# A gated graph layer on one core: the edges' scan cut into sixteen parts and placed in other units, the edge table's later steps moved

## What is computed

```python
h = relu(layernorm(x))
u = h @ root + bias
for r in range(8):
    mask = (edge_type == r)
    sums = segment_sum(h[src] * mask, dst)      # one row per node
    cnt  = segment_sum(mask, dst)
    u = u + (sums / max(cnt, 1)) @ weight[r]
z = concat([u, h]) @ w_gate + b_gate
out = x + tanh(u) * z + h * (1 - z)
```

## Time and profile before

| | |
|---|---|
| time, three runs | 1409.28, 1410.62, 1416.18 us; median 1410.62 |
| the profiled execution: span from the first to the last instruction | 1407.7 us |
| busy: TensorE matmuls | 1291.5 us, 92% of the span |
| busy: VectorE | 952.5 us, 68% |
| busy: GpSimd | 754.8 us, 54% |
| busy: ScalarE | 409.0 us, 29% |
| the chain that ended last, by engine | PE 61%, DVE 13%, DMA 10%, issue 7%, POOL 4%, ACT 2% |

### The profile page before, as it was taken

One profiled execution on the slowest core, in us unless ns is written; L12 is line 12 of the kernel. 1 busy time (PEld: TensorE's weight loads), 2 busy tenths in 40 slices (PEclk: granted clock), 3 DMA queues, 4 the chain that ended last, 5 costly groups with the idle time before them and its releaser, 6 DMA issues.

```text
span 1407.7 us, 20144 instructions
## 1 busy us (share of the span) xinstructions
PE 1291.5 (92%) x6205; PEld 651.6 (46%) x6205; DVE 952.5 (68%) x1260; ACT 409.0 (29%) x501; POOL 754.8 (54%) x837
## 2 busy tenths in 40 slices
PE   2978899999999999999998999998999989786898
PEld 1434344444444445555554445454445445343565
DVE  6889678366565667775675577646666778765777
ACT  5344123214132422321332043223222323432000
POOL 2423088786878426686687558664756464320000
PEclk9998899999999999999999999999999999998999
DMA  6442125215224348777875887769889977648872
GB/s 220 154 173 101 44 52 156 69 45 171 54 59 122 114 158 277 238 237 247 277 209 161 292 267 246 238 210 305 279 254 303 312 230 240 204 138 248 239 226 90
DMA packets 112355, 269.44 MB, mean 191 GB/s; under 512 B 22558, under 2 KB 23061, under 8 KB 112268
## 3 DMA queue, kind: packets, MB, share of 16 engines
q1 hardware_dynamic: 78284, 185.88, 40.2%
q0 software_dynamic: 33984, 82.40, 20.4%
HBM read 203.66 MB, written 87.30 MB: 207 GB/s over the span
## 4 chain that ended last, share of the span: by engine, by line
PE 61%; DVE 13%; DMA 10%; issue 7%; POOL 4%; ACT 2%; DVEq 1%; SPq 1%; POOLq 1%; ACTq 0%
PE ps L1320 52%; PE ps L1278 8%; DMA early<-y_rows,pair 7%; DVE W L937 2%; DMA early<-u_rows 1%; POOL onehot L641 1%; DVE hT L990 1%; DMA W<-in_L_gnn_weight_dram 1%; POOL early L633 1%; DVE hT L985 1%; PE ps L1313 1%; POOL pair L623 1%; DVE early L1147 1%; DVE early L1069 1%; DVE early L1163 1%
## 5 line engine op out<-in xcount | busy, mean ns | idle before, releaser
L1320 PE MATMUL ps<-W,hT 128*128 128x512 f16 (+2 forms) x4740 | 1076.0, 385 | 13.0 <-DVE W L937 13.0
L1320 PEld LDWEIGHTS ps<-W,hT 128*128 128x128 f16 (+2 forms) x4740 | 479.9, 104 | 537.8 <-issue 43.4
L633 POOL DMA_INDIRECT early<-y_rows,pair x200 | 242.1, 1211 | 194.5 <-PE ps L1281 152.4
L606 POOL DMA_INDIRECT table_rows<-edges,table_i x160 | 240.5, 1503 | 100.6 <-issue 100.6
L1278 PE MATMUL ps<-early,onehot 128*125 x800 | 205.9, 385 | 26.6 <-POOL onehot L641 13.1
L641 POOL TENSOR_SCALAR onehot<-iota_d,pair 128x125 f16<-128x125 f16 x185 | 159.9, 864 | 64.2 <-DMA early<-y_rows,pair 58.2
L766 ACT ACTIVATE yhl<-early 128x512 f16<-128x512 f32 x120 | 75.3, 628 | 355.3 <-DVE early L1069 194.2
L937 DVE SCALAR_TENSOR_TENSOR W<-W,wsc 128x2048 f16<-128x2048 f32 x62 | 146.5, 2364 | 13.8 <-ACT W L716 13.7
L1278 PEld LDWEIGHTS ps<-early,onehot 128*125 x800 | 106.8, 137 | 100.4 <-issue 46.6
L716 ACT ACTIVATE W<-W,wsc 128x2048 f16<-128x2048 f32 x62 | 122.6, 1990 | 50.9 <-DVE wsc L932 20.3
L683 ACT ACTIVATE peek_out<-W 128x1024 bf16<-128x1024 f32 x80 | 84.2, 1052 | 94.7 <-DMA W<-in_L_gnn_weight_dram 72.7
(11 more groups left out here) (184 smaller groups left out, 756.0 us busy)
## 6 DMA issues: line engine op xcount, KB each, us to landing
y_rows<-yhl SPq DMA_DIRECT2D x144, 256.0 KB
W<-in_L_gnn_weight_dram SPq DMA_DIRECT2D x31, 1024.0 KB, 7.4
early<-u_rows SPq DMA_DIRECT2D x52, 448.0 KB
u_rows<-early SPq DMA_DIRECT2D x50, 448.0 KB
W<-in_L_gnn_w_gate_dram SPq DMA_DIRECT2D x8, 1024.0 KB, 8.3
early<-in_x_dram SPq DMA_DIRECT2D x9, 512.0 KB, 4.5
hs_rows<-early SPq DMA_DIRECT2D x9, 512.0 KB, 3.2
u_rows<-yhl SPq DMA_DIRECT2D x18, 256.0 KB
```

The costliest lines, as they stand in the source:

```text
L606: pool.indirect_dma_start(out=table_rows, out_offset=bass.IndirectOffsetOnAxis(ap=at_i[:, c:c + 1], axis=0), in_=packed[0:EP, c:c + 1], in ...
L633: pool.indirect_dma_start(out=G[:, b, :], out_offset=None, in_=y_rows[i], in_offset=bass.IndirectOffsetOnAxis(ap=idx[:, b, :], axis=0), bo ...
L1320: last = nc.tensor.matmul(ps[0:rows, n % 4, :], hT[:, m, v_h, k, n0:n0 + rows], Wh[MAT[w][c]][:, v_w, k, :], start=(first and v_h + v_w == ...
```

## The change

The scan over 80 groups is done in 16 parts of 5 groups in place of 4 parts of 20, and the parts stand in other steps. `totals`, `group_bounds` and `positions` move to later steps. Inside a step, `positions` now comes behind `low_weights`. GpSimd fills all the scan's factors after its second `split_low`, in place of one quarter after each of the third to the sixth.

```diff
     SQ = 4
-    KEYS_AT, SCAN_AT, TOTALS_AT, BOUNDS_AT = 2, {4: 0, 7: 1, 10: 2, 12: 3}, 14, 16
-    POSITIONS_AT = {18: 0, 22: 1, 26: 2, 30: 3}
+    SN = 16
+    KEYS_AT, TOTALS_AT, BOUNDS_AT = 2, 18, 20
+    SCAN_AT = {6: (0, 1), 8: (2,), 9: (3,), 11: (4, 5), 12: (6,), 13: (7, 8), 14: (9,), 15: (10, 11), 16: (12, 13), 17: (14, 15)}
+    POSITIONS_AT = {22: 0, 25: 1, 28: 2, 32: 3}
...
             for i in range(NJ):
                 split_low(i)
-                if 2 <= i <= SQ + 1:
-                    scan_factors(i - 2)
+                if i == 1:
+                    for b in range(SQ):
+                        scan_factors(b)
...
             def scan_part(b):
-                g0, g1 = b * NG // SQ, (b + 1) * NG // SQ
+                g0, g1 = b * NG // SN, (b + 1) * NG // SN
...
-                dve.wait_ge(s["factors_ready"], 2 * (b + 1))
+                dve.wait_ge(s["factors_ready"], 2 * (b * SQ // SN + 1))
...
-                dve.wait_ge(s["scan_ready"], SQ)
+                dve.wait_ge(s["scan_ready"], SN)
...
-                if n in SCAN_AT:
-                    scan_part(SCAN_AT[n])
+                for b in SCAN_AT.get(n, ()):
+                    scan_part(b)
...
-                if n in POSITIONS_AT:
-                    positions(POSITIONS_AT[n])
...
                 for w, c in LOWS.get(n, ()):
                     low_weights(w, c)
+                if n in POSITIONS_AT:
+                    positions(POSITIONS_AT[n])
...
             def totals():
-                pe.wait_ge(s["scan_ready"], SQ)
+                pe.wait_ge(s["scan_ready"], SN)
```

More of the change, by code:

```diff
@@ L158, in gated_rgcn_preln @@
     SQ = 4
-    KEYS_AT, SCAN_AT, TOTALS_AT, BOUNDS_AT = 2, {4: 0, 7: 1, 10: 2, 12: 3}, 14, 16
-    POSITIONS_AT = {18: 0, 22: 1, 26: 2, 30: 3}
+    SN = 16
+    KEYS_AT, TOTALS_AT, BOUNDS_AT = 2, 18, 20
+    SCAN_AT = {6: (0, 1), 8: (2,), 9: (3,), 11: (4, 5), 12: (6,), 13: (7, 8), 14: (9,), 15: (10, 11), 16: (12, 13), 17: (14, 15)}
+    assert [b for n in sorted(SCAN_AT) for b in SCAN_AT[n]] == list(range(SN))
+    POSITIONS_AT = {22: 0, 25: 1, 28: 2, 32: 3}
     TABLE_AT = AGG_AT[0] - 4
```

## The result

| | before | after |
|---|---|---|
| median, 13 runs each | 1407.72 us | 1392.9 us (1377.15 to 1398.16) |
| ratio after to before | | 0.9882 (95% interval 0.9851 to 0.9913) |
| profiled span | 1407.7 us | 1393.1 us |

The change makes the kernel 1.2% faster. The ratio leaves out one slow run of the kernel after (1398.16 us), so it is not the quotient of the two medians (0.9895). Lines after are numbered higher than before by 3 or 4: L606 is now L610 (scatters), L915 L919, L937 L941, L985 L989, L990 L994, L1278 L1282.

What follows compares the result with a forecast made beforehand. TensorE, busy 92% of the span, bounds; only its waits can be won. 32.2 - 3 - 1.6 = 27.6 us at unit 20, of which 18.7 remain at unit 109: span 1389.0, median 1391.9; range 1381 to 1404, likeliest 1386 to 1397.

Steps and rivals of the forecast that it cites:

- the early gaps: Four TensorE waits up to unit 20, two near 4.82 us, then 5.45 and 7.06; 32.2 us winnable there.
- `totals` waits: After unit 18, totals waits for VectorE's queue: 2.8 us counted, 3 taken, bounds 0 and 8.4.
- the way from the table to the sum: Table load, table, first gather, first sum at unit 109, priced from rows before; chain end 486.6, sum 502.0 us.
- The long scan was a hold: Quarter scans of 8.63 us instead of 6.83 were read as held beside a GpSimd split, not slow.
- I take 1.6: At the start, VectorE's L915 is held until the running memset ends, so all starts 1.6 us late.
- the rival's size: Memsets hold the start in full, 4.4 us: 2.8 more than summed, time 1395; no chance of its own given.
- collisions: Scatters held beside VectorE instructions with two SBUF inputs; they lengthen the scatter chain by 5.7 us, bounds -2.3 and 14.
- POOL's gathers, which only repeat this wait: At unit 109, the gathers were named among the next late, as only repeating TensorE's wait of 8.6 us.
- The quick chain: Rival: fewer scatters held, TensorE finds the table ready; gain 27 to 29 us, time 1382 to 1384; chance 0.17.
- The scan fits: Opposite of a rival: scan parts slow or bringing back a wait, gain 11 to 12 us, time 1399; chance 0.22.
- Slower: Rival: the scatter chain is the new bound, mean scatter above 2.0 us; at 2.14, time 1424; chance 0.09.
- Set by units, gathers and loads that all move with it: After unit 109, everything moves with the first sum, so its 18.7 us gain lasts to the span's end.

Runs made afterwards that it cites:

- e10: The kernel after, unchanged, run once more with a profile; 1381.41 us.
- e11: The kernel after, unchanged, run a further time with a profile; 1385.92 us.
- e5: The kernel after with the scan in four quarters again, in steps 6, 9, 13 and 16; median 1389.75 us, ratio to before 0.9886.
- e6: The kernel before with only the later steps of totals, group_bounds and positions and the low halves ahead of positions; 1398.91 us, ratio to before 0.9944.
- e1: The kernel after, but GpSimd waits with the memsets until weight 0's scale is made; median 1385.89 us, ratio to before 0.9838.
- e8: The kernel after plus 24 unread VectorE products with two SBUF inputs inside the scatter chain; 1393.53 us, one run.
- e9: The kernel after plus 24 unread VectorE reductions with one SBUF input inside the scatter chain; 1381.10 us, one run.
- e2: The kernel after with the factors' memsets back where the kernel before had them, a quarter after splits 3 to 6; 1384.55 us, one run.
- e3: The kernel after with group_bounds after unit 19 and the first positions in step 20 instead of 22; median 1378.39 us, ratio to before 0.978.
- e4: The kernel after with the first positions in step 20 and the memsets waiting for weight 0's scale; median 1377.1 us, ratio to before 0.978.
- e7: The kernel after, but GpSimd waits for each quarter's fill to be written before starting the next; 1389.64 us, one run.

## Why the prediction was right

Predicted 1392.0, measured 1392.9. The mechanism came out as predicted: the early gaps go, the chain of scatters takes over, TensorE waits at the first sum. The terms one by one, in the profile after and in two more executions of the same kernel:

| term | predicted | profile after | e10, e11 |
|---|---|---|---|
| start held by the memsets | 1.6 us | 4.4 | 1.9, 4.3 |
| a scan part | 1.02 + 1.86 us | 0.98 + 1.82 | the same |
| `totals` waits | 3 us | 1.30 | 1.30, 1.31 |
| unit 20 taken out | 157.1 | 158.79 | 154.78, 157.16 |
| first scatter | 178.3 | 180.05 | 176.05, 178.43 |
| chain of scatters | 308.3 us | 305.3 | 303.6, 301.9 |
| its end to the first gather | 9.2 us | 11.4 | 12.3, 8.8 |
| gather to first sum | 6.1 us | 8.6 | 8.4, 9.7 |
| wait there | 8.6 us | 10.09 | 10.86, 5.32 |
| first sum | 502.0 | 505.31 | 500.39, 498.92 |
| gain at the first sum's start | 20.4 us | 17.1 | 22.0, 23.5 |
| the clock behind the wait | 1.7 us | 1.4 | 2.2, 2.1 |
| left at the end of the span | 18.7 us | 14.6 | 28.1, 23.5 |

**Luck in the last digit.** That the totals agree within 1 us is chance. The prediction took 18.7 us off 1410.62, a median of three runs; over 13 runs the median before is 1407.72, and the two medians differ by 14.8. Of the 2.9 us that it puts between span and time only some 1.7 lie around the span (1394.83 and 1393.1 in the profiled run after), the rest is a difference between runs. And in the profile after, errors offset one another: the start was 2.8 us later than taken and the way from the table to the sum 4.7 longer, `totals` waited 1.7 less and the chain was 3.0 shorter.

**The long scan was a hold,** as read there. With the parts away from the splits all 16 scans take 1.82 us, and in e5 all four quarters 6.82 to 6.83; in e6, in the old steps, three of the four take 8.62 to 8.63 again.

**Mis-sized: "I take 1.6".** The profile after shows the rival's size, a hold to the end of all memsets. e10 shows the size taken, in another execution of the same kernel. So not the row chosen was wrong, but that there is one value. The upper one was a rival with a price of its own, 1395. `totals` waits 1.30 us with the long hold (after), the short one (e10) and none (e1), so its 3 us were mis-sized on their own. The Trainium skill (SBUF — State Buffer, "Who interferes with whom") says that a `tensor_scalar` in a two-port mode and GpSimd shut each other out, for the whole instruction of the one that issued first. The trace agrees in that L919 is held by an instruction that GpSimd had begun; how long in a chain of them is not in the rule, and in which mode L919 ran no run shows.

**Right place, other sum: collisions.** The estimate was 7 more held scatters at 1.14 us, less two (2.3 us) for the low halves that run earlier: +5.7. Counted over the 160 scatters, 36 took more than 1.5 us before and 42 do after, in all three profiles, and the busy time of all grew from 240.7 to 248.5 us (246.4 and 245.2 in e10 and e11), by 4.5 to 7.8: as a size of the collisions, 5.7 was good. What the sum left out is the idle time between scatters, which fell by 4.7 to 5.1 us (one of 6.34 before is not there after). So the chain changed by -0.7 to +2.7 us, not by +5.7. That two-input instructions of VectorE are the cause was argued from single rows in the prediction; e8 and e9 show it.

**Taken as unchanged, and not: the way from the table to the sum.** It was priced from the rows before, where the table lay ready 28 us early. On the path, in the profile after, the table's load took 1.8 us longer, GpSimd's copy was held for 1.25, and the gather took 2.5 longer to the sum. "POOL's gathers, which only repeat this wait" was thus priced too low. SyncE's timeline after, and one line of it before, show what ran beside these rows:

```profile
487.06 1.62 SPq L415 DMA_DIRECT2D early<-u_rows  x4
496.57 26.04 SPq L390 DMA_DIRECT2D W<-in_L_gnn_weight_dram  x3
```

```profile
518.81 2.59 SPq L387 DMA_DIRECT2D W<-in_L_gnn_weight_dram  x2
```

The table's load landed in 4.3 to 5.4 us in the five profiles in which SyncE issued four loads of `u` 0.4 us ahead of it (after, e1, e2, e9, e10), and in 2.6 to 3.0 in the other eight. And VectorE's L941, the low half behind `table`, sets free the buffer for the next weight, whose load SyncE issues as L941 ends. From the first gather to the first sum it is 6.1 us where GpSimd's record of the gather ends 1.5 us ahead of this load (before, e3, e4; there the gathers waited for the store of `y`), and 8.4 to 9.8 in all other profiles, where the load goes out first, by 0.9 to 1.3 us. In four of these (e5, e6, e7, e11) L941 also held the gather itself:

```profile
489.19 3.19 POOL L637 DMA_INDIRECT early<-y_rows,pair  x1 [0.72 <-POOL pair L627]
```

This is e11's; in the profile after it took 1.10 us. That the two kinds of load delay the landings is the likeliest reading of 13 profiles, but it is not shown: no run moves a load alone.

**Rivals.** The quick chain did not happen (TensorE waited); it is what e3 makes. The scan fits: no part beside units with statistics brought a wait. Slower: the mean scatter (305.3 / 160 = 1.91 us) stayed under the 2.0 at which it would have decided (its price of 1424 leaves out the clock's 1.7, which the sum has); e8, at 1.97, has 9.8 us of gain left at that place (512.54 against 522.38), where e9 has 20.6.

**After unit 109** the lead shrinks from 17.1 to 14.6 us at the span's end in the profile after, grows from 22.0 to 28.1 in e10 and stays at 23.5 in e11. "Set by units, gathers and loads that all move with it" is thus borne out only to within some 6 us, by which executions of one kernel differ there.

## What to carry to other kernels

When gaps of the bounding engine are removed, follow what it will wait for next, and count that chain from the moved start: here the scatters started no earlier than before, and 28 us of cover turned into a wait of 10. Starting that chain two units earlier (e3) was worth, by the medians, nearly as much again as the whole change. Price a side chain that comes onto the path anew, since every row of it was measured while nobody waited for it.

## What the runs showed of the hardware

- A small VectorE instruction (`tensor_scalar`, 128 columns, 0.29 us) beside back-to-back memsets of GpSimd takes 1.65 or 4.55 us, in executions of the same program: it ends with the memset that was running or with the last of the chain.
- A GpSimd scatter that takes 1.19 us alone took 2.25 us more beside a VectorE instruction with two SBUF inputs (e8); 24 reductions of the same length as e8's products left the chain as it was (305.4 us, against 301.9 to 305.3).
- Behind the wait of 10 us, in which TensorE did nothing, the granted clock is low. The first line below gives busy time of TensorE and the other engines, granted clock (third from the end) and DMA in the 10 us from the first sum on, in the kernel after: the clock is 0.85 as a mean of the two levels (1.2 and 2.4 GHz). The first sum (1.96 us) and the twelve matmuls behind it (0.27 us each) take 1.4 us more than the next ones.

```profile
505.00:515.00 10.00, 9.69 (x42) 4.95 (x43) 3.05 (x5) 0.00 (x0) 7.40 (x13) 0.85 0.84 266
```

```profile
507.13 3.20 PE L1324 MATMUL ps<-W,hT 128*128 128x512 f16 x12
510.17 1.03 PE L1282 MATMUL ps<-early,onehot 128*125 x4
...
511.06 2.75 PE L1324 MATMUL ps<-W,hT 128*128 128x512 f16 x12
```
